# Stage 0 narrowed to one batch, the other states prepared inside the first two pairs, and the biases moved into a weight row (two-block transformer layer, one core)

## What is computed

```
_layernorm(x) = (x - mean(x)) / sqrt(var(x) + 1e-5)        # over the 128 features, no gain, no bias

h     = _layernorm(x)
q,k,v = tanh(h @ Wq + bq), tanh(h @ Wk + bk), tanh(h @ Wv + bv)      # Wq, Wk, Wv: [128, 1024]
ctx   = causal softmax(q k^T / 8) v                                   # per batch and head
x     = x + _layernorm(tanh(ctx @ Wo + bo))
x     = x + _layernorm(latent attention and experts of _layernorm(x))
```

## Time and profile before

| | |
|---|---|
| median of 3 runs | 1772.61 us (1771.38 to 1773.12) |
| the profiled execution | 1779.43 us, of which its span 1777.6 us |
| busy, share of the span | PE 92%, DVE 81%, ACT 69%, POOL 22% |
| TensorE matmuls | 14930 |
| mean granted TensorE clock | 0.954 of full speed |

### The profile page before, as it was taken

How to read it: one execution, slowest core, us unless ns; L and a number is a source line. 1 busy time by engine, 2 the same in 40 slices (tenths; PEclk the granted TensorE clock), 3 DMA queues, 4 the chain that set the end, 5 groups by cost and what they waited for, 6 DMA issues and landing times. The chain is left out here.

```text
span 1777.6 us, 39595 instructions
## 1 busy us (share of the span) xinstructions
PE 1640.0 (92%) x14930; PEld 715.8 (40%) x14930; DVE 1437.1 (81%) x2115; ACT 1218.6 (69%) x1185; POOL 384.3 (22%) x506
## 2 busy tenths in 40 slices
PE   2899999999999999984999999998999999889995
PEld 1344444444444444432223233322332332366774
DVE  5377777888888888887898899897989999267888
ACT  3566666666666666643787777786778788756776
POOL 6211112333333333323401000100010212120004
PEclk8899999999999999995899899998999999979998
DMA  4311101100000000002002000200020010000001
GB/s 135 68 54 38 37 37 38 38 36 37 37 37 37 37 25 32 20 4 60 25 25 49 13 13 25 46 17 15 25 42 20 13 37 13 13 2 13 13 12 47
DMA packets 48154, 57.13 MB, mean 32 GB/s; under 512 B 9406, under 2 KB 34462, under 8 KB 48032
## 3 DMA queue, kind: packets, MB, share of 16 engines
q1 hardware_dynamic: 46988, 53.71, 10.2%
q10 hardware_dynamic: 1044, 1.76, 0.3%
HBM read 15.07 MB, written 10.49 MB: 14 GB/s over the span
## 5 line engine op out<-in xcount | busy, mean ns | idle before, releaser
L1472 DVE TENSOR_REDUCE arena<-psum 128x2 f32<-128x1024 f32 x490 | 580.9, 1220 | 57.2 <-PE psum L1121 53.0
L1298 ACT ACTIVATE arena<-psum 128x1024 f32<-128x1024 f32 x512 | 522.7, 1024 | 151.9 <-PE psum L1091 137.5
L652 ACT ACTIVATE arena<-psum 128x2048 f32<-128x2048 f32 (+1 forms) x160 | 273.3, 1708 | 232.8 <-PE psum L537 230.0
L1106 PE MATMUL psum<-arena 128*32 128x256 f32 x4096 | 333.9, 398 | 2.5 <-issue 0.7
L554 PE MATMUL psum<-arena,hs 128*64 128x512 f32 (+3 forms) x1536 | 283.0, 496 | 2.7 <-POOL arena L701 2.2
L701 POOL TENSOR_SCALAR_AFFINE_SELECT arena<-arena 128x512 f32<-128x512 f32 (+1 forms) x160 | 167.8, 1066 | 535.2 <-ACT arena L652 535.2
L1121 PE MATMUL psum<-arena 32*128 32x512 bf16 x1068 | 210.1, 408 | 24.7 <-ACT arena L1351 12.0
L537 PE MATMUL psum<-arena 64*128 64x512 f16 (+3 forms) x2304 | 216.3, 325 | 4.9 <-DVE arena L738 3.6
L1091 PE MATMUL psum<-arena 32*128 32x512 bf16 x1024 | 202.2, 392 | 4.4 <-issue 2.9
L738 DVE TENSOR_TENSOR arena<-arena 128x1024 f16<-128x1024 f32 x64 | 78.4, 1225 | 139.4 <-ACT arena L631 139.4
L554 PEld LDWEIGHTS psum<-arena,hs 128*64 128x64 f32 x1536 | 96.1, 136 | 144.8 <-issue 125.7
(11 more groups left out here) (202 smaller groups left out, 2123.8 us busy)
## 6 DMA issues: line engine op xcount, KB each, us to landing
arena<-arena SPq DMA_DIRECT2D x32, 512.0 KB, 3.0
arena<-arena SPq DMA_DIRECT2D x48, 128.0 KB, 2.3
arena<-latent_q SPq DMA_DIRECT2D x64, 64.0 KB, 2.0
arena<-latent_k SPq DMA_DIRECT2D x64, 64.0 KB, 2.0
arena<-arena SPq DMA_DIRECT2D x32, 96.0 KB, 2.6
X<-in_L_attn_states SPq DMA_DIRECT2D x4, 512.0 KB, 13.5
arena<-arena SPq DMA_DIRECT2D x32, 64.0 KB, 1.8
out_x<-X SPq DMA_DIRECT2D x4, 512.0 KB, 3.2
```

The source lines that it names most:

```text
L652: nc.scalar.activation(probs[g], SC[:, :, 0:WIDTH[g]], ACT.Exp, scale=DH ** -0.5).then_inc(exp_done, 1)
L1106: last = nc.tensor.matmul(OT[ROWS * c:ROWS * (c + 1), h * HALF // 2:(h + 1) * HALF // 2], v_cols[par][:, kt, 2 * pr + i, :], e_probs[u % 4 ...
L1298: nc.scalar.activation(e_probs[u % 4], src, ACT.Exp, scale=KD ** -0.5).then_inc(e_done, 1)
L1472: nc.vector.tensor_reduce(half_tops[:, kh, qt, 2 * pr:2 * pr + 2], src.rearrange("p (i c) -> p i c", i=2), AX.X, ALU.max).then_inc(top_don ...
```

## The change

1. **Biases in row 0.** `xT` gets row 0 = 1: `hs[:, :, 0]` and `acc[:, :, 0]` are set to 1.0 by POOL and only features 1 to 127 are normalised into them. Row 0 of W is subtracted from rows 1 to 127 and its place is taken by the bias. For this the ACT queue loads rows 1 to 127 of Wv, Wq, Wk into partitions 1 to 127 of `w_in`; the SP queue loads row 0 of each, repeated, into partitions 1 to 127 of a second tile `w_first`, and the three biases into partition 0 of `w_in`; DVE subtracts (`less_first`, three of 128x1024 f32) and ACT rounds only then. `less_first(0)` waits for all nine loads.
2. **Gone with it:** the fourth product of `values` (8 per pair), the bias operand of the four tanh per pair, `pick_bias`, `vbias`, `bias_in`, `qk_bias` and their loads and small steps.
3. **Stage 0 prepares batch 0 alone.** SP issues its other three state loads and `Wo` last. Moments of batches 1 to 3 and their normalising (now all on DVE, into `acc`) come first in DVE's stage 1, around `low_part(0, .)`; `Wo` is split by POOL at its start of stage 1. PE transposes batch 1 and 2 in pair 0 and batch 3 in pair 1 (`turn_normal`, 8 transposes each, through PJ), ACT and DVE split them there (`states_hi`, `states_lo`).
4. **`acc` is filled with `bo`** by ACT, batch by batch (`begin_acc`), not by POOL.
5. **Pairs 0 and 1 read `xT_all` and `W_all` directly;** their SBUF copies are gone.

```diff
-QSLOT, KSLOT, VSLOT, OSLOT, NSLOT = 0, 2, 4, 7, 9
+QSLOT, KSLOT, VSLOT, OSLOT, NSLOT = 0, 2, 4, 6, 8
...
+        def norm_states(dve, b):
+
+            dve.wait_ge(rstd0, b + 1)
+            for t in range(b * T, (b + 1) * T):
+                last = nc.vector.tensor_scalar(normal_states(b)[:, t, 1:], X[:, t, 1:], mv[:, t, 0:1], rstd[:, t:t + 1],
+                                               ALU.subtract, ALU.mult)
...
-                for b in range(B):
+                def load_states(b):
                     sp.dma_start(X[:, b * T:(b + 1) * T, :], x_dram[:, b * T:(b + 1) * T, :]).then_inc(x_in[b], 16)
-                sp.dma_start(wo_in0, Wo.rearrange("(n r) d -> r n d", n=PAIRS)).then_inc(wo_got, 16)
+
+                load_states(0)
+                for t, w in ((2, Wv), (0, Wq), (1, Wk)):
+                    sp.dma_start(w_first[1:P, t, :], w[0, :].partition_broadcast(P - 1)).then_inc(first_got, 16)
+                for t, bias in ((2, bv), (0, bq), (1, bk)):
+                    sp.dma_start(w_in[0:1, t, :], bias.rearrange("(a n) -> a n", a=1)).then_inc(first_got, 16)
...
-                for t, w in enumerate((Wq, Wk, Wv)):
-                    act.dma_start(w_in[:, t, :], w).then_inc(w_got, 16)
...
+                for t, w in ((2, Wv), (0, Wq), (1, Wk)):
+                    act.dma_start(w_in[1:P, t, :], w[1:P, :]).then_inc(w_got, 16)
...
+                def less_first(k):
+                    t = (2, 0, 1)[k]
+                    if k == 0:
+                        dve.wait_ge(first_clear, 1)
+                        dve.wait_ge(w_got, 16 * 3)
+                        dve.wait_ge(first_got, 16 * 6)
+                    nc.vector.tensor_tensor(w_in[:, t, :], w_in[:, t, :], w_first[:, t, :], ALU.subtract).then_inc(w_less, 1)
...
+                state_moments(dve, 0)
+                less_first(0)
+                dve.wait_ge(consts, 2)
+                norm_states(dve, 0)
+                less_first(1)
+                less_first(2)
+                for k in range(3):
+                    weights_lo(k)
+                states_lo(dve, 0, bank(0, 2))
...
-                        last = nc.tensor.matmul(o, pick_bias, w_v[par][:, 2, :], start=False, stop=True)
...
+                    else:
+                        pe.wait_ge(tanh_done, 8)
+                        turn_normal(pe, 1, PJ)
                     scores(i, 4, par)
                     context(i, 3, par)
                     if at_least(i, 2):
                         output(i - 2, par)
+                    elif i == 1:
+                        pe.wait_ge(den_read, 2)
+                        turn_normal(pe, 3, PJ)
+                    else:
+                        pe.wait_ge(xt_lo, 2)
+                        turn_normal(pe, 2, PJ)
```

More of the change, by code:

```diff
@@ L173, in build, with state_moments @@
         d0, p0, a0s = sem("d0"), sem("p0"), sem("a0s")
-        shift_half, shift_done, xn_act = sem("shift_half"), sem("shift_done"), sem("xn_act")
         rstd0, xn0, xt_ps, xt_hi, xt_lo = sem("rstd0"), sem("xn0"), sem("xt_ps"), sem("xt_hi"), sem("xt_lo")
[L176 to L181, removed]
+        biasT_ps, whi_done, mv0 = sem("biasT_ps"), sem("whi_done"), sem("mv0")
+        def state_moments(dve, b):
+            steps = Steps(dve, d0)
+            steps.n = b * T
+            dve.wait_ge(x_in[b], 16)
+            for t in range(b * T, (b + 1) * T):
+                steps.done(nc.vector.bn_stats(stats[:, t, :], X[:, t, :]))
             steps.now()
@@ L223, in _ @@
[L223 to L241, removed]
@@ L278, in _ @@
-                pool.wait_ge(wo_split, 3)
             @block.vector
             def _(dve):
-                steps = Steps(dve, d0)
-                steps.done(nc.vector.memset(pick_bias, 0.0))
-                steps.now()
-                for row in (0, 32):
-                    steps.done(nc.vector.memset(pick_bias[row:row + 1, :], 1.0))
-                for e in range(E):
-                    nc.vector.memset(iota_e[:, e:e + 1], float(e))
-                for b in range(B):
-                    dve.wait_ge(x_in[b], 16)
-                    norm_stats(dve, steps, lambda t: X[:, b * T + t, :], b).then_inc(mv0, 1)
@@ L343, in build @@
         w_qk = [a1b.take(4 * P // 2, F16).rearrange("p (j c) -> p j c", j=4) for _ in range(2)]
[L344 removed]
+        w_v = [a1b.take(2 * P // 2, F16).rearrange("p (j c) -> p j c", j=2) for _ in range(2)]
         w_o = [a1b.take(2 * D // 2, F16).rearrange("p (j d) -> p j d", j=2) for _ in range(2)]
@@ L686, in pair, with begin_acc, take_states @@
                     exp(i, 3)
+                    if not at_least(i, 1):
+                        take_states(1)
                     exp(i, 4)
+                    if not at_least(i, 2):
+                        take_states(2 + i)
+                def begin_acc(b):
+                    nc.scalar.activation(acc[:, b * T:(b + 1) * T, :], bo_b[:, :].unsqueeze(1).to_broadcast([P, T, D]), ACT.Copy,
+                                         scale=WSCALE).then_inc(acc_begun, 1)
+                def take_states(b):
+                    states_hi(act, b, PJ)
+                    begin_acc(b)
+                nc.scalar.copy(b1T[:, :], bank(7)[:, 0:E * FC]).then_inc(a0s, 1)
+                nc.scalar.copy(b_lat[:, :], bank(7)[:, E * FC:E * FC + 1]).then_inc(a0s, 1)
+                begin_acc(0)
+                for t in range(2):
+                    half = slice(t * LAT, (t + 1) * LAT)
+                    nc.scalar.copy(w_lat[:, half].rearrange("p (g d j) -> p g d j", g=GROUPS, d=KD),
+                                   w_lat_in[:, half].rearrange("p (g j d) -> p g d j", g=GROUPS, d=KD)).then_inc(a0s, 1)
                 value_tanh(0, 0)
@@ L867, in pair @@
                         scale_ctx(i - 1, 1 - par)
+                for b in range(1, B):
+                    state_moments(dve, b)
+                dve.wait_ge(consts, 6)
+                norm_states(dve, 1)
                 low_part(0, 0, 0)
+                norm_states(dve, 2)
                 low_part(0, 1, 0)
+                norm_states(dve, 3)
                 each_pair(dve, pair)
```

181 lines of the change are left out of this document (86 added, 95 removed).

## The result

The changed kernel takes **1858.55 us** (median of 4 runs, 1853.78 to 1869.47) against 1772.86 us (4 runs) of the kernel before on the same chip: a ratio of 1.048, with an interval of 1.0443 to 1.0517. That is 85.7 us slower; the forecast was 1860, in a range of 1838 to 1892. The profiled execution took 1869.47 us, its span 1867.4, the longest of the four.

A forecast was written before the change was run, and what follows sets the result against it. Loads and preparation were taken to bound the first 42.20 us, PE the time from 126 us on. 99.5 - 0.9 - 3.5 - 11.4 + 3.3 = +87.0 on the profiled 1779.4 gives 1866.4; the median, 6.8 lower, 1860, range 1838 to 1892.

The forecast's parts named there:

- One lane for 127 rows: Stage 0 loads: each of the six 127-row loads uses one DMA lane, the same for both queues, 127 being prime.
- both queues end together: Stage 0 loads: the SP and ACT queues feed one lane, so their loads finish at the same time.
- 765 packets x 166 ns = 127.0, less_first at 130.9: Stage 0: 6x127 + 3 packets of 4 KB on one lane take 127.0 us, so the first subtraction starts at 130.9.
- 10.5 us of DVE, 0.3 to the next block: End of stage 0: subtractions, normalising and low parts on DVE take 10.5 us, then the next block starts 0.3 us later.
- Stage 0 +99.5: Whole of stage 0: first `values` product at 141.7 us in place of 42.2, +99.5 us.
- Pairs 0 to 4, -0.9 and +3.3: Start of stage 1: pair 0's shorter `values` saves 0.9 us; transposes and other changes in pairs 0 to 2 add 3.3.
- DVE's moments and normalising are done in time: even: Pair 0: the moved moments and first normalising, 8.9 us on DVE, end when tanh is ready, costing nothing.
- Pairs 4 to 12, -3.5: Stage 1, 8 intervals with PE never idle: dropping the fourth product saves 3.5 us, 0.44 a pair.
- Pairs 12 to 31, -11.4: Normalising pairs, 19 intervals: 0.44 us from the fourth product and two times 0.08 from tanh, 0.60 each, 11.4 saved.
- rival 3: Stage 1: the gain does not come, PE waiting elsewhere; at most 15 us more, 1875; a fifth of the one-lane case's 0.88.
- Behind stage 1, 0: The stages after stage 1 are unchanged, so they add nothing to the sum.
- Rival 1: Stage 0: the loads use all 16 lanes, first `values` at 24.5, kernel 1742 us; decides from four lanes on; chance 0.07.

## Why the prediction was right

- **One lane for 127 rows** (from the 130 completion writes of the earlier trace rows and the 12- and 20-row stores of the earlier trace rows): right. The DMA's share until the end of the loads and less_first, released by a DMA, were where one lane puts them, and a cut alone gives the time back. That both queues end together was wrong, without harm to the sum: ACT's queue has no 4 KB packet left from 112 us on, and SP's runs to 126.
- **765 packets x 166 ns = 127.0, less_first at 130.9:** 126.5. From 2.6 us + 1.3 us of states on, that is 160 ns a packet, 3.5% cheaper. The 141 ns estimated from the 27 GiB/s of the Trainium skill ("DMA: Bandwidth & Descriptors", section "Specifications") would have come out 15 us too low.
- **10.5 us of DVE, 0.3 to the next block:** 10.1 and 0.9, the 0.5 of SP's tail in it. Together 11.0 for 10.8.
- **Stage 0 +99.5:** +95.3. Nearly all of the difference is the packet.
- **Pairs 0 to 4, -0.9 and +3.3:** +1.1 and +1.9, so +3.0 for +2.4. Two errors hide in it: "DVE's moments and normalising are done in time: even" failed (POOL's `Wo` split beside it costs 2.4 to 2.9 us, and I had called that split hidden), and the transposes take 1.09 us a group, not 1.5. The two pull in opposite directions, so that the sum is only 0.6 off is partly luck, and the base is not firm either: the kernel before ran the 18.67 us of its pair 0 at a granted clock of 0.50, while the kernel without the bias operand ran the same 63 products in 15.20 us at 0.84.
- **Pairs 4 to 12, -3.5:** -4.2. An interval went from 22.73 to 22.31, as the product asks; the last of the eight already belongs to the normalising pairs and lost 1.2.
- **Pairs 12 to 31, -11.4:** -12.7; an interval 0.67 shorter instead of 0.60. Both parts were confirmed alone (0.44 and 0.18). The wait of PE that I left at half its size is gone. So rival 3, no gain in stage 1, is refuted.
- **Behind stage 1, 0:** +8.4 in the profiled execution, at a clock of 0.93 for 0.94. The four runs go from 1853.78 at a mean clock of 0.968 to 1869.47 at 0.958, and their median is 85.7 above before where the sum says 87.0. The terms come to 81.4 without this stretch and to 89.8 with it, the medians to 85.7. The interval of the ratio, 78.5 to 91.7 us, holds all three, so an agreement within 1.3 us is closer than the runs can tell.
- **Rival 1, all lanes, 1742:** its condition was false, but its price was tested: 1745.15 with a cut, less_first 5 us late for a reason the prediction didn't know; uncut, less_first at 14.05 against the 12 assumed. "It decides from four lanes on" was right: three lanes are even.

## What to carry to other kernels

Dropping or sparing one partition of a load can cost far more than the row is worth: count the lanes of each load from its rows before the bytes, and load the full 128 rows, then overwrite the one that must differ, if the overwriting isn't itself in the chain (here it gave back 2.9 of 4.7 us). A load that holds a queue also holds every issue behind it, so small loads may be better ahead of a long one; that was not tried here. And read what a moved POOL step runs beside: a step that nobody waits for can still make a step of DVE late that somebody waits for.

## What the runs showed of the hardware that was not expected

- **Cut loads are slow on all lanes.** 4 KB packets take 162 to 167 ns in uncut 128-row loads and 230 to 310 ns in loads cut 112 + 15, 7 + 120 or 120 + 8; 401 GB/s against 229 to 267. Neither the rows a lane, nor the repeated row, nor the start partition is the reason; what is stays open.
- **DVE and POOL hinder each other.** Eight normalising steps take 0.34 us each alone; beside POOL's `Wo` split the longest took 2.29 (line L201, 147 to 154 us):

```profile
L201 DVE TENSOR_SCALAR acc<-X,mv,rstd x8: 334/968/2286, 147.3 to 151.2; 128x127 f32<-128x127 f32 x8
```

  and three steps of POOL, 6.8 us, lie in the same stretch. The Trainium skill ("SBUF — State Buffer", section "Who interferes with whom") names a pair of ports that the two share and that an instruction holds to its end. The longest step ended at 153.46, just behind POOL's subtraction (151.26 to 153.38), which agrees. But three of the eight took 0.33 us while POOL's scaling was recorded as running (146.44 to 150.07); a pair held through that whole step would not have let them pass.
- **Copies within SBUF of 16 rows by 12 KB** need 1.9 us for each row, 6.4 GB/s a lane in place of the 24.7 of the 128-row copies in the earlier trace rows, so eight of them cost more than the 1.5 MB from memory that they replaced.
